# A vision-transformer tower on one Trainium2 core: the split of the score maxima moved from VectorE to GpSimd, and one 48-column transpose in place of four

## The reference, cut to what matters

```
h = layernorm(h + attn0(h)); h = layernorm(h + ffn0(h))     # layer 0: window of +-64 keys
h = layernorm(h + attn1(h)); h = layernorm(h + experts(h))  # layer 1: causal, top-2 of 8 experts
attn: scores = q k^T / 4 ; masked ; probs = softmax(scores, axis=keys) ; out = probs v
```

## Time and profile before

| | |
|---|---|
| runs | 998.98, 999.82, 1000.0 us |
| the profiled execution | 999.01 us, its span 997.1 us |
| granted TensorE clock, mean | 0.922 |
| PE busy | 855.4 us (86% of the span) |
| DVE busy | 542.0 us (54%) |
| ACT busy | 421.5 us (42%) |
| POOL busy | 304.6 us (31%) |
| attention and dense phases | 0 to about 640 us |
| experts and last layernorm | about 640 to 997 us |

### The profile page before, as it was taken

One profiled execution on the slowest core, in us unless ns is written; L12 is line 12 of the kernel. 1 busy time (PEld: TensorE's weight loads), 2 busy tenths in 40 slices (PEclk: granted clock), 3 DMA queues, 4 the chain that ended last, 5 costly groups with the idle time before them and its releaser, 6 DMA issues. The chain is left out here.

```text
span 997.1 us, 14099 instructions
## 1 busy us (share of the span) xinstructions
PE 855.4 (86%) x4842; PEld 541.8 (54%) x4842; DVE 542.0 (54%) x2095; ACT 421.5 (42%) x741; POOL 304.6 (31%) x365
## 2 busy tenths in 40 slices
PE   6979999898898899899889798349999999999940
PEld 2655556545455455355445243236877877877830
DVE  1268535779798799799878777410211211210136
ACT  1315434587585586686455556113021021022005
POOL 6113223434334333222253423460203212302332
PEclk9998999999799799899799689669999999999975
DMA  9652211202202202201321301631145135233242
GB/s 345 207 188 65 59 29 48 81 1 66 65 2 65 65 1 65 66 23 44 86 84 43 106 7 61 223 116 43 16 127 143 22 122 143 27 120 71 27 110 84
DMA packets 57510, 81.48 MB, mean 82 GB/s; under 512 B 6624, under 2 KB 51041, under 8 KB 55008
## 3 DMA queue, kind: packets, MB, share of 16 engines
q1 hardware_dynamic: 49520, 70.48, 22.0%
q0 software_dynamic: 7296, 9.47, 5.7%
q10 hardware_dynamic: 624, 0.63, 0.2%
HBM read 35.37 MB, written 19.68 MB: 55 GB/s over the span
## 5 line engine op out<-in xcount | busy, mean ns | idle before, releaser
L1102 DVE CUSTOM_DVE_ANT_0 junk<-ps,maskb 128x256 bf16<-128x256 f32 (+4 forms) x512 | 205.8, 434 | 66.3 <-PE ps L821 64.9
L647 ACT ACTIVATE probs<-ps 128x512 f32<-128x512 f32 (+1 forms) x304 | 157.4, 552 | 95.6 <-PE ps L844 91.3
L1559 PE MATMUL ps<-dxT,qs 128*128 128x320 f32 x512 | 141.1, 436 | 1.3 <-DVE dxT L1633 1.3
L1571 PE MATMUL ps<-ks,hTe 128*128 128x256 f32 x640 | 139.3, 379 | 0.0
L1593 ACT ACTIVATE hTe<-ps,qs 128x640 f32<-128x640 f32 x64 | 50.8, 793 | 204.6 <-PE ps L1559 204.6
L1515 POOL DMA_INDIRECT mixed_rows<-ysb,ids x40 | 61.7, 1543 | 228.1 <-DVE ysb L1653 225.2
L1571 PEld LDWEIGHTS ps<-ks,hTe 128*128 128x128 f32 x640 | 121.1, 190 | 16.3
L1559 PEld LDWEIGHTS ps<-dxT,qs 128*128 128x128 f32 x512 | 97.9, 192 | 42.5 <-DVE dxT L1633 1.9
L844 PE MATMUL ps<-qs,ks 99*128 99x256 bf16 (+4 forms) x512 | 107.7, 296 | 15.3 <-DVE nmax L1102 9.0
L821 PE MATMUL ps<-ks,qs 96*128 96x256 bf16 (+4 forms) x512 | 108.8, 299 | 12.6 <-DVE nmax L1102 7.3
L860 PE MATMUL ps<-probs,vaug 128*32 128x256 f32 (+4 forms) x1024 | 92.6, 437 | 6.2 <-POOL probs L557 5.6
(11 more groups left out here) (188 smaller groups left out, 1193.0 us busy)
## 6 DMA issues: line engine op xcount, KB each, us to landing
qs<-parts SPq DMA_DIRECT2D x96, 128.0 KB, 2.4
ks<-parts SPq DMA_DIRECT2D x96, 128.0 KB, 2.4
qs<-w SPq DMA_DIRECT2D x8, 1024.0 KB, 9.5
ks<-w SPq DMA_DIRECT2D x8, 1024.0 KB, 4.9
dispatched_rows<-att SPq DMA_DIRECT2D x8, 650.0 KB, 10.4
ks<-dispatched_rows SPq DMA_DIRECT2D x4, 650.0 KB, 7.2
x_sb<-xT SPq DMA_DIRECT2D x8, 256.0 KB, 3.9
mixed_rows<-h SPq DMA_DIRECT2D x4, 512.0 KB, 3.3
```

The source lines that it names most:

```text
L647: act.activation(probs_of(u)[:, heads[0]:heads[-1] + 1, :], turned_bank((u, half, i))[:, 0:len(heads) * w].rearrange("p (j n) -> p j n", n=w),
L1102: ins = dve.tensor_tensor_reduce(out=junk[:, b - (b > V_BANK), a * (hi - lo):(a + 1) * (hi - lo)], in0=score_bank((u, half, i))[:, a * (hi ...
L1559: ins = mm(bank(2 * (n % 2) + c)[:, 0:HC], w1s[:, e % 2, k, m * P:(m + 1) * P], dxT[:, e % 2, k, c * HC:(c + 1) * HC], start=(k == 0), sto ...
L1571: ins = mm(bank(4 + n % 2)[:, 0:D], hTe[:, e % 2, m, t * P:(t + 1) * P], w2s[:, e % 2, m, :], start=(m == 0), stop=(m == MH - 1))
```

## The change

POOL gets a function `split_maxima(g)` with all four split operations of a group, one behind the other, at half step 8g+8 and ahead of `select(4g-4)`. It waits for the last maximum of the group, for the transposes of group g-2 (which read the same buffer), and between its own operations on a semaphore. DVE loses the four operations; at its first maximum of a group it now waits until the split of group g-2 is done, since `nmax` has two buffers. `nparts` is laid out as part, head, tile, so that one transpose with 48 columns gives 48 rows of 128; before, four transposes of 12 columns gave 12 rows of 512. ACT copies 48x128 in place of 12x512, and the DMA moves 48 pieces of 256 bytes in place of 12 of 1024.

```diff
@@ vector @@
-                                if split is not None:
-                                    split_maxima(split[0], split[1] + n)
...
+                        if t == 0 and half == 0 and g >= 2:
+                            dve.wait_ge(nparts_done, g - 1)
@@ gpsimd @@
+                    def split_maxima(g):
+                        full = nmax[:, g % 2, :, :]
+                        dst = nparts[:, g % 2, :, :, :]
+                        u = NT * g + NT - 1
+                        pool.wait_ge(*s_out((u, 1, len(score_heads(u, 1)) - 1)))
+                        if g >= 2:
+                            pool.wait_ge(*t_full(("n", g - 2)))
+                        pool.tensor_copy(dst[:, 0, :, :], full).then_inc(max_chain, 1)
+                        pool.wait_ge(max_chain, 3 * g + 1)
+                        pool.tensor_tensor(nrest[:, :, :], full, dst[:, 0, :, :], ALU.subtract).then_inc(max_chain, 1)
+                        pool.wait_ge(max_chain, 3 * g + 2)
+                        pool.tensor_copy(dst[:, 1, :, :], nrest[:, :, :]).then_inc(max_chain, 1)
+                        pool.wait_ge(max_chain, 3 * g + 3)
+                        pool.tensor_tensor(dst[:, 2, :, :], nrest[:, :, :], dst[:, 1, :, :],
+                                           ALU.subtract).then_inc(nparts_done, 1)
...
                     for eta in HALVES:
+                        if eta % 8 == 0 and 0 < eta <= 2 * UNITS:
+                            split_maxima(eta // 8 - 1)
@@ scalar @@
-                        act.activation(nrows[:, g % 2, :], turned_bank(("n", g)).bitcast(BF16)[0:3 * HG, 0:S],
+                        act.activation(nrows[:, g % 2, :], turned_bank(("n", g)).bitcast(BF16)[0:3 * HG * NT, 0:P],
...
-                        act.dma_start(qs[KS:KM, r, h0:h0 + HG, :], nrows[:, g % 2, :]).then_inc(nmax_in[g % 2], 16)
+                        act.dma_start(qs[KS:KM, r, h0:h0 + HG, :].rearrange("c j (t n) -> c (j t) n", n=P),
+                                      nrows[:, g % 2, :]).then_inc(nmax_in[g % 2], 16)
@@ tensor @@
-                        for t in range(NT):
-                            ins = pe.transpose(o.bitcast(BF16)[0:3 * HG, t * P:(t + 1) * P], nparts[:, g % 2, t, :],
-                                               identb[:, :])
-                        ins.then_inc(t_full(("n", g))[0], 1)
+                        pe.transpose(o.bitcast(BF16)[0:3 * HG * NT, 0:P],
+                                     nparts[:, g % 2, :, :, :].rearrange("p c j t -> p (c j t)"),
+                                     identb[:, :]).then_inc(t_full(("n", g))[0], 1)
```

More of the change, by code:

```diff
@@ L297, in build @@
             sem(n) for n in ("pv_mm", "ot_done", "sel_done", "nparts_done", "max_chain"))
+        head_chain = sem("head_chain")
         nmax_in = [sem(f"nmax_in{i}") for i in range(2)]
@@ L350, in build @@
             nrest = sb2("nrest", [P, HG, NT])
-            nparts = sb2("nparts", [P, 2, NT, 3 * HG], BF16)
-            nrows = sb2("nrows", [3 * HG, 2, S], BF16)
+            nparts = sb2("nparts", [P, 2, 3, HG, NT], BF16)
+            nrows = sb2("nrows", [3 * HG * NT, 2, P], BF16)
             junk = sb2("junk", [P, BANKS - 1, S], BF16)
@@ L1078, in link @@
                         chained[n] += 1
-                        ins.then_inc((ln_chain, q_chain, fh_chain, w_chain, max_chain, route_chain)[n], 1)
+                        ins.then_inc((ln_chain, q_chain, fh_chain, w_chain, head_chain, route_chain)[n], 1)
                     def linked(n):
-                        dve.wait_ge((ln_chain, q_chain, fh_chain, w_chain, max_chain, route_chain)[n], chained[n])
+                        dve.wait_ge((ln_chain, q_chain, fh_chain, w_chain, head_chain, route_chain)[n], chained[n])
                     dve.memset(wsc[:, :], 0.0).then_inc(prep, 1)
@@ L1088, in _, with maximum @@
                     dve.tensor_copy(trib[:, :], cst[:, C_TRI:C_TRI + 2 * P]).then_inc(prep, 1)
-                    def maximum(u, half, split):
+                    def maximum(u, half):
                         g, t = divmod(u, NT)
+                        if t == 0 and half == 0 and g >= 2:
+                            dve.wait_ge(nparts_done, g - 1)
                         lo, hi = k_range(kind_of(u), t)
@@ L1096, in maximum @@
                             mask = maskb[:, c:c + hi - lo]
-                        n = 0
                         for i, heads in enumerate(score_heads(u, half)):
@@ L1437, in _ @@
                             heads(e // 8)
-                        e = eta - 8
-                        split = (e // 8, 2 * (e % 8)) if e >= 0 and e % 8 < 2 and e < 2 * UNITS else None
                         if 0 <= eta < 2 * UNITS:
[L1441 to L1444, removed]
+                            maximum(*divmod(eta, 2))
                         for step in SCHED.get(eta, ()):
```

## The result

| | before | changed |
|---|---|---|
| median of six runs beside one another | 999.4 us | 993.1 us (991.77 to 995.44) |
| ratio, 95% interval | 1 | 0.9943 [0.9925, 0.9961] |
| the profiled execution, its span | 999.01, 997.1 us | 992.61, 990.7 us |
| granted clock, mean | 0.922 | 0.923 |

The account below looks back on a forecast made before the run. In the attention stage PE sets the pace, DVE is close behind and POOL has room. From the profiled execution, 999.01 - 4.2 - 5 + 2.1 = 991.9 us; range 984 to 1000, leaving no more than 2 in 10 out.

Parts of the forecast that it names:

- PE, -4.2 us: Three transposes fewer per group on PE, 0.06 us each, counted for 23/32 of groups: -4.2 us, bounds -2 and -8.
- The rival in which saved transposes turn into waits: PE is bound by DVE all through, so only the DVE part counts: 996 us; chance 0.1.
- DVE, -5 us: Four operations fewer per group in DVE's queue shorten PE's waits for DVE: -5 us of 5.7, bounds -2 and -10.
- its 3.7 us at the transposes go whole: PE's 3.7 us of waiting at the transposes for DVE's late split disappear entirely.
- 2 more go behind L1288: Of PE's 3.3 us wait for the hidden layer's product on DVE, about 2 us disappear.
- nothing at the maxima: Of PE's 16.2 us of waits for maxima nothing is credited; most come half a group after the split.
- POOL, +2.1 us: POOL's 1.04 us split chain delays PE at groups 24 and 28, behind late sends: +2.1 us, bounds +1.6 and +8.6.
- At nothing: ACT's shorter copy (0.3 us per group) and the DMA's 48 packets (0.1 to 0.15 us more) are covered, counting nothing.
- The rival of the long chain: POOL's four operations cost about 1 us each: 1003.4 us; decides from a chain of about 3.5 us; chance 0.07.
- Contention: New POOL operations hold DVE up, losing more than the 17 us freed: 996.2 us; chance 0.12.
- The clock: PE's mean granted clock shifts in the stage: a 0.02 fall gives 1000.8 us, chance 0.1; a rise 983, chance 0.06.
- the prediction's own price: A fall of 0.02 in the stage's mean clock, over 530 us at 90% busy, costs some 9 us.

Follow-up runs that it names:

- e1: Kernel before with one 48-column transpose per group, short ACT copy and 48-piece DMA, split still on DVE: 0.9961 of the kernel before.
- e6: Changed kernel, with DVE still doing its four split operations at their old places, into tiles nobody reads: 0.9980 of the kernel before.
- e3: Changed kernel with the sends spread, one indirect DMA per half step in place of two: 0.9817 of the kernel before, 981.92 us.
- e10: Kernel before with one transpose per group, split still on DVE, and sends spread to one indirect DMA per half step: 0.9875 of the kernel before.
- e4: Kernel before with only the sends spread, one indirect DMA per half step in place of two: 0.9904 of the kernel before, 991.11 us.
- e2: Changed kernel without its transpose change: POOL splits, in the old layout with four 12-column transposes: 0.9982 of the kernel before.
- e5: Changed kernel with 4 idle copies on POOL ahead of each split, chain 2.1 us: 0.9974 of the kernel before.
- e7: Changed kernel with 12 idle copies on POOL ahead of each split, chain 4.2 us: 1.0133 of the kernel before.
- e9: Changed kernel with 12 idle POOL copies ahead of each split, chain 4.2 us, and spread sends: 1.0038 of the kernel before.

## Why the prediction was right, and where its reasons were not

The forecast was 991.9 us, 7.9 below the median; the changed kernel has 993.1, and 5.7 us less by the ratio. The sum of the terms was -7.1, and the interval of the result reaches from -3.9 to -7.5. The 7.9 came of subtracting that sum from one execution 0.8 us below the median.

**PE, -4.2 us: right.** e1 removes the transposes alone and gives -3.9 [-2.5, -5.3]. The rival in which saved transposes turn into waits is refuted: e1's waits are those of before.

**DVE, -5 us: the size fits, the reason was wrong.** e6 against the change gives 3.7 us, give or take 2, for the four operations in DVE's queue, and e3 against e10 gives 5.8 for the move as a whole. In groups 1 to 23, before any send, the change gains 10.1 and 11.6 us (e3, the same program there, 11.6), and e1 with e10 6.0 and 5.8: a difference of about 5. But the prediction had it that "its 3.7 us at the transposes go whole", that 2 more go behind L1288, and nothing at the maxima. The step that failed is this attribution of the gain to named waits. The wait for DVE at the transposes went and the one behind L1288 shrank from 3.3 to 2.2 us, yet PE's waits in all did not shrink. Groups 1 to 23 (columns as in the earlier trace rows), before:

```profile
90.43:492.93 402.50, 366.06 (x2493) 207.83 (x2493) 317.36 (x1224) 253.11 (x448) 134.50 (x198) 0.93 0.18 49
```

The changed kernel, and e6:

```profile
92.82:483.68 390.86, 354.12 (x2411) 201.66 (x2426) 304.41 (x1135) 246.33 (x448) 152.60 (x286) 0.95 0.19 51
94.22:489.70 395.48, 357.92 (x2412) 202.90 (x2427) 315.40 (x1223) 246.50 (x448) 153.36 (x286) 0.94 0.18 50
```

PE stands idle for 402.50 - 366.06 = 36.4 us before, for 36.7 with the change (36.8 in its repetition) and 37.6 in e6. The 11.6 us that the change gains here are busy time. The transposes are 3 to 4 us of it (22 groups at 0.39 - 0.24 us, or at 3 x 0.057). The rest goes along with the clock: PE is at the lower level for 54.5 us of this stretch before, 38.2 with the change and 49.4 in e6, and 16 us less of half the clock are worth up to 8. e6 then loses its 3.7 us as the clock goes, with 0.918 in the mean for 0.923, and not in waits.

Two things keep this from being a rule. Part of it is chance: e4 is the program of before up to group 23, and it has 46.6 us at the lower level for 54.5. And e1, whose DVE queue is as full as that of e6, has a mean clock of 0.921. Taken together, the five kernels with the four operations on DVE are at the lower level there for 43.9 to 54.5 us, the eight without them for 37.6 to 44.9. How DVE's queue acts on the clock, when PE waits as long in total, stays open. Nor can the gain be read as shorter waits in the row of the maxima: that row grew from 16.2 to 19.1 us.

**POOL, +2.1 us: right as to mechanism and place; its size can't be told closely.** The chain is 1.07 us for 1.04. PE's waits for POOL grew by 2.6 us (5.6 to 8.2). In groups 23 to 31 the change loses 1.8 and 2.8 us, e2 2.7, and e1 gains 0.1. By the ratios, e6 against e1 says 1.9 give or take 2, the two gains by spreading (e3, e4) 3.0 give or take 3, and the four kernels of e10's comparison 4 give or take 3. All include 2.1; the centre of them is higher, about 3. The forecast had PE's wait growing by 1.04 us at each send, and it grew by 1.15 and 1.48.

**At nothing: right.** PE waited for no copy of `nrows`; one wait for the DMA of 1.8 us remains, and e4, with the old DMA of 12 pieces, has one of 1.7.

**The rival of the long chain** was right in its direction and wrong in its point. It was to decide from 3.5 us on. The cost is 3 us for the first doubling and 16 more for the next (2.1 to 4.2 us). On the straight line between e5 (-2.6) and e7 (+13.3), the gain is used up at about 2.4 us; as the cost bends upward, somewhat above. The prediction had looked at groups 24, 28, 29 and 31 alone. For 29 and 31 it had 2.5 us each, and e7 shows 2.5 and 2.8; what it missed are six other groups with 4.1 us of waits together, and that it priced each wait at its own length.

**Contention** is refuted: with 27 us more on POOL, and 107 in e7, the durations on DVE stand. The contention of before went where the operations went: now the longest cast on POOL takes 658 ns, for 997 on DVE, and it ends within 0.1 us of an operation on DVE (L1306) that began just ahead of it. That agrees with what the Trainium skill says (SBUF — State Buffer, "Who interferes with whom") of operations that block each other whoever starts first; the maxima, 201 us of DVE's 524, read PSUM and one mask, and take 435 ns in the mean, 434 before.

**The clock** did not take it back: 0.923 for 0.922 over the span. But within the stage it moved both ways, 0.95 for 0.93 from 100 to 500 us and 0.86 for 0.90 from 500 to 600. At the prediction's own price (0.02 over 530 us for 9 us) the first is worth some 7 us and the second costs 3. That the two, with the 2.4 us lost ahead of group 1, nearly cancel is luck: the forecast has no term for either.

## What to carry to other kernels

Price an operation that is given to an engine with much idle time at the few places where that engine's queue is late, and look at what stands ahead of it there: here eight indirect DMAs of about 1.28 us each (0.97 and a pause of 0.30) made 27 us of cheap work cost 2 to 4 us, and spreading them over twice the half steps gained more (12.6 us) than the change itself (5.7). When work leaves an engine that another keeps waiting for, do not credit the wait that stands nearest to it. The gain shows as progress per group, while the rows of waits may even grow; compare busy time, idle time and granted clock over the same groups before giving it a cause.

## What was not expected of the hardware

A wait of PE cost more than its own length. In e3 6.6 us of waits for POOL went and 12.6 us of time, in e4 4.3 and 9.6; in e7 PE waited 14.3 us longer for POOL than in the change, and the time grew by 19; in e9 against e3, 14.9 and 22. The granted clock goes along. Between 500 and 600 us it is 0.93 in e3, 0.86 in the change and 0.81 in e7. Between the starts of groups 1 and 31 PE is at the lower level, 1.2 GHz, for 54.6, 68.3 and 88.7 us in that order. Time at half the clock is time in which PE gets half as much done. So the 13.7 us less of it in e3 are worth up to 7 us, of the 6 that the waits leave unexplained, and the 20.4 us more in e7 up to 10, of some 5. That the waits are what brings the clock down is a reading of these kernels side by side; no run sets the clock and the waits apart.

One program shows the tie of time and clock by itself. Of e2's twelve executions, the four at a mean clock of 0.926 are 2 to 5 us shorter than the eight at 0.921 to 0.923.

Open: why the stretch at the lower clock at about 74 us is 6.8 us long in some executions and 10.2 or 13.7 in others, which is worth 2 to 3 us; and why e6 is granted less than e1.
